# Squares through DRAM from the first step, and the keys' trip issued from ScalarE

## The reference

```python
# attention part (attention-free transformer with a local band)
emb = layernorm(x) + ctx
q, k, v = emb @ wq + bq, emb @ wk + bk, emb @ wv + bv
ek = exp(k - max(k)); ew = exp(w - max(w))        # w: pos_bias inside a band of 64
y = sigmoid(q) * (ew @ (ek * v)) / (ew @ ek)
a = layernorm(y @ wo + bo + emb) * gamma + beta                       # "mid"
ff = relu(a @ w1 + b1) @ w2 + b2
x1 = x + tanh(g_xattn) * (layernorm(ff + a) * gamma + beta)           # "ff"
# channel-mixing part, on xn = layernorm(x1)                          # "fin"
r = sigmoid(mix(xn, mu_r) @ Wr.T); kk = relu(mix(xn, mu_k) @ Wk.T) ** 2
out = x1 + tanh(g_ffn) * r * (kk @ Wv.T)          # mix blends a row with the one before it
```

## Time and profile before

| | |
|---|---|
| time, median of 3 runs | 459.03 us (458.91 to 459.86) |
| the profiled execution | 458.91 us, its span 457.1 us |
| mean granted TensorE clock | 0.996 of full speed |
| TensorE matmul busy | 435.7 us, 95% of the span |
| VectorE, ScalarE, GpSimd busy | 380.0, 286.0, 286.1 us |

### The profile page before, as it was taken

How to read it: one execution, slowest core, us unless ns; L and a number is a source line. 1 busy time by engine, 2 the same in 40 slices (tenths; PEclk the granted TensorE clock), 3 DMA queues, 4 the chain that set the end, 5 groups by cost and what they waited for, 6 DMA issues and landing times.

```text
span 457.1 us, 8142 instructions
## 1 busy us (share of the span) xinstructions
PE 435.7 (95%) x2892; PEld 394.4 (86%) x2892; DVE 380.0 (83%) x768; ACT 286.0 (63%) x449; POOL 286.1 (63%) x227
## 2 busy tenths in 40 slices
PE   8989989997999999999999999999999999998975
PEld 8778789996988888998889888998889898987975
DVE  4998869987597979799798979799788876598887
ACT  3683563835687578745967487745965478537453
POOL 2586847571878657894878657894868453753611
PEclk9999999999899999999999999999999999999999
DMA  8840330442215750448215650445213330011002
GB/s 275 280 138 2 106 103 2 129 125 81 93 55 169 190 150 5 138 128 208 92 56 170 189 145 9 139 127 162 95 58 122 102 101 1 0 48 46 3 0 93
DMA packets 43497, 47.23 MB, mean 103 GB/s; under 512 B 8512, under 2 KB 39744, under 8 KB 43456
## 3 DMA queue, kind: packets, MB, share of 16 engines
q1 hardware_dynamic: 42368, 45.13, 32.6%
q10 hardware_dynamic: 1088, 1.57, 1.0%
HBM read 30.76 MB, written 15.93 MB: 102 GB/s over the span
## 4 chain that ended last, share of the span: by engine, by line
POOL 33%; issue 28%; DVE 15%; PE 11%; ACT 10%; DMA 2%; SPq 0%; POOLq 0%; DVEq 0%; ACTq 0%
PE ps L1806 10%; POOL ek_lo L240 5%; POOL ev_lo L240 5%; POOL x_beta L626 3%; POOL xk_lo L240 2%; POOL emb L352 2%; POOL a_rows L626 2%; POOL rs_mid L618 2%; POOL rs_fin L618 2%; POOL nmr_fin L621 1%; POOL rs_ff L618 1%; DVE ps L948 1%; DVE xk L1031 1%; DVE xr L1031 1%; POOL rs_head L618 1%
## 5 line engine op out<-in xcount | busy, mean ns | idle before, releaser
L1806 PE MATMUL ps<-w_hi,hid_hi 128*128 128x256 f32 x248 | 62.2, 286 | 0.8 <-issue 0.5
L1806 PE MATMUL ps<-w_lo,hid_hi 128*128 128x256 f32 x248 | 61.7, 285 | 0.0
L1595 ACT ACTIVATE hid_hi<-ps,b 128x512 fp32r<-128x512 f32 x60 | 37.7, 681 | 23.6 <-PE ps L1806 23.6
L1806 PE MATMUL ps<-a_hi,w_hi 128*128 128x512 f32 x128 | 50.9, 397 | 1.1 <-DVE hid_lo L1108 1.1
L240 POOL TENSOR_TENSOR ek_lo<-y,ek_hi 128x1024 fp32r<-128x1024 f32 x13 | 36.2, 2788 | 24.5 <-DVE xr L1031 17.8
L1806 PE MATMUL ps<-a_hi,w_lo 128*128 128x512 f32 x128 | 50.7, 396 | 0.0
L1806 PEld LDWEIGHTS ps<-w_hi,hid_hi 128*128 128x128 f32 x248 | 47.6, 192 | 1.7 <-issue 1.2
L1806 PEld LDWEIGHTS ps<-w_lo,hid_hi 128*128 128x128 f32 x248 | 47.5, 192 | 0.3
L1108 DVE SCALAR_TENSOR_TENSOR hid_lo<-ps,neg_b,hid 128x512 fp32r<-128x512 f32 x60 | 41.3, 736 | 3.2 <-ACT hid L1601 3.2
L1601 ACT ACTIVATE hid<-hid_hi,neg_b 128x512 f32<-128x512 f32 x60 | 40.0, 722 | 0.0
L240 POOL TENSOR_TENSOR ev_lo<-res,ev_hi 128x1024 fp32r<-128x1024 f32 x8 | 19.1, 2392 | 29.7 <-ACT ev_hi L1509 29.7
(11 more groups left out here) (278 smaller groups left out, 1407.8 us busy)
## 6 DMA issues: line engine op xcount, KB each, us to landing
x_in<-in_x SPq DMA_DIRECT2D x8, 512.0 KB, 4.6
emb<-in_ctx SPq DMA_DIRECT2D x8, 512.0 KB, 4.3
x_beta<-in_x SPq DMA_DIRECT2D x8, 512.0 KB, 4.3
out<-out_sb SPq DMA_DIRECT2D x7, 512.0 KB, 4.3
key_room<-norm SPq DMA_DIRECT2D x6, 512.0 KB, 2.6
y<-key_room SPq DMA_DIRECT2D x24, 128.0 KB, 2.9
fin_room<-xk SPq DMA_DIRECT2D x6, 512.0 KB, 2.6
out_sb<-fin_room SPq DMA_DIRECT2D x24, 128.0 KB, 2.9
```

The lines of the kernel that those rows point to most:

```text
L1595: act.activation(tile(hi, b, T), bank(relu_pair(n, q), b), ACT.Relu, bias=b1[:, m:m + 1]).then_inc(hid_hi_done, 1)
L1806: return pe.matmul(o, s, m, start=start, stop=stop, skip_group_check=True)
```

## The change

Step 1 now sends the mid rows of batch 1 by squares: TensorE's eight transposes go, and its `queries(2)` move to their place. VectorE turns the mid squares right after their normalisation, and turns the keys' squares after that rather than before. The key squares' round trip is issued from ScalarE's list (`spread_first_keys`), with a semaphore of its own. SP's list of the step now has the load of ctx, the mid trip, the embeddings, the load of x, and the small sums last. VectorE's list of the step is put in another order, `ek_high(2)` on ScalarE comes after `choose_log`, and GpSimd's `stats("ff")` comes ahead of `ek_low(2)`. Three row constants (`bias_rows`, `gamma_t`, `beta_t`) are made by VectorE instead of GpSimd, and two small ones later than before.

```diff
-FIRST_MID = 2
+FIRST_MID = 1
@@ SP, step 1
-                if i == 1:
-                    spread_keys(i + 1)
+                if i == FIRST_MID:
                     load_ctx(i + 2, p)
-                    spread_sums(i + 1)
+                    spread_mid(i)
                     store_emb(i + 2)
                     load_x(i + 3)
                     load_emb(i + 2)
+                    spread_sums(i + 1)
                     load_again(i)
                     spread_fin(i - 1)
@@ GpSimd, prologue and step 1
-            pool.tensor_tensor(bias_rows, bias_rows, beta_t, ALU.add).then_inc(row_const, 1)
-            pool.tensor_scalar(gamma_t, gamma_t, gates[:, 0:1], None, ALU.mult).then_inc(row_const, 1)
-            pool.wait_ge(row_const, 2)
-            pool.tensor_scalar(beta_t, beta_t, gates[:, 0:1], None, ALU.mult).then_inc(row_const, 1)
...
+                stats("ff", b)
                 ek_low(pool, d)
-                stats("ff", b)
                 stats("fin", b)
@@ VectorE, turn_key_squares
-                dve.wait_ge(mid_turned, mid_turns(n - 2))
-                dve.wait_ge(a_scaled_done, 1)
+                dve.wait_ge(mid_turned, mid_turns(max(n - 2, FIRST_MID)))
+                dve.wait_ge(a_scaled_done, 2 if n == FIRST_EK else 1)
@@ VectorE, prologue
             keep_values(1, 3)
+            dve.wait_ge(act_const, 4)
+            dve.tensor_tensor(bias_rows, bias_rows, beta_t, ALU.add).then_inc(dve_const, 1)
+            dve.tensor_scalar(gamma_t, gamma_t, gates[:, 0:1], None, ALU.mult).then_inc(dve_const, 1)
+            dve.wait_ge(dve_const, 2)
+            dve.tensor_scalar(beta_t, beta_t, gates[:, 0:1], None, ALU.mult).then_inc(dve_const, 1)
...
             keys_low(1)
@@ VectorE, step 1
                 head_stats(e)
-                turn_key_squares(d)
                 unit_low(6)
+                unit_low(7)
                 attention_sum(i, p)
                 hidden_low(b, 2)
-                unit_low(7)
                 normalise_mid(i)
+                turn_mid_squares(i)
                 hidden_low(b, 3)
+                turn_key_squares(d)
+                turn_emb_squares(e, p)
+                ff_sum(b, 1 - p)
                 sum_keys(d)
-                a_low(i)
-                ff_sum(b, 1 - p)
-                turn_emb_squares(e, p)
                 ff_stats(b)
+                a_square_low(dve, i)
                 scale_ff(b)
                 keep_values(d)
+                finish_x1(b)
                 weigh_values(d)
+                fin_stats(b)
                 sums_low(d, 0)
                 hidden_low(i, 0)
-                finish_x1(b)
-                fin_stats(b)
                 hidden_low(i, 1)
@@ ScalarE
+            def spread_first_keys():
+                act.wait_ge(ek_turned, FIRST_EK + DC)
+                act.dma_start(key_room.rearrange("(p n) -> p n", p=P), ek_blocks).then_inc(key_room_filled, 16)
+                act.wait_ge(key_room_filled, 16)
+                act.wait_ge(y_lo_done, FIRST_EK)
+                for b in range(NB):
+                    act.dma_start(ek_square[SQ * b:SQ * (b + 1)].rearrange("i (a n) -> i a n", a=NB),
+                                  key_room.rearrange("(a i b n) -> b i a n", a=NB, i=SQ, b=NB)[b]).then_inc(ek_landed, 16)
@@ ScalarE, step 1
                 normalise("mid", i, res)
-                ek_high(d)
+                spread_first_keys()
                 a_high(i)
                 act.wait_ge(act_const, 2)
                 exp_q(d, 2)
                 choose_log()
+                ek_high(d)
                 hidden_high(i, 0)
@@ TensorE, step 1
                     add_hidden(b, 3, rest=False)
-                    pe.wait_ge(norm_done["mid"], TT * (i + 1))
-                    turn(2, norm, mid_turned)
+                    pe.wait_ge(res_done, i + 1)
+                    queries(d, 2)
                     add_hidden(b, 3, high=False)
                 relus_read(NQ * i)
                 values(d, 1)
-                if not has(a):
-                    pe.wait_ge(a_lo_done, i + 1)
-                    queries(d, 2)
                 hidden(i, 0, DC * i)
```

More of the change, by code:

```diff
@@ L168, in flamingo_gated_block @@
         ident_set, const_set, dve_const, act_const = sem("ident_set"), sem("const_set"), sem("dve_const"), sem("act_const")
-        row_const = sem("row_const")
         w_hi_done = sem("w_hi_done")
@@ L210, in flamingo_gated_block @@
                                                                       sem("emb_landed"), sem("fin_landed"))
-        room_filled = sem("room_filled")
+        room_filled, key_room_filled = sem("room_filled"), sem("key_room_filled")
         log_done, guess_done, inverse_done = sem("log_done"), sem("guess_done"), sem("inverse_done")
@@ L292, in stored @@
         def stored(step, place):
-            return 16 * (place if step == 1 else 4 + 5 * (step - 2) + place)
+            return 16 * (place if step == FIRST_MID else 4 + 5 * (step - FIRST_MID - 1) + place)
         def keys_stored(n):
@@ L300, in mid_stored @@
         def mid_stored(n):
-            return stored(n, 2)
+            return stored(n, 1 if n == FIRST_MID else 2)
         def sums_stored(n):
-            return stored(n - 1, 2 if n == FIRST_EK else 3)
+            return stored(n - 1, 3)
         def emb_stored(n):
-            return stored(n - 2, 3 if n == FIRST_EMB else 4)
+            return stored(n - 2, 2 if n == FIRST_EMB else 4)
         def fin_stored(n):
@@ L320, in mid_turns @@
         def mid_turns(n):
-            return n + 1 if n < FIRST_MID else FIRST_MID + DC * (min(n, BATCH - 2) + 1 - FIRST_MID) + (n == BATCH - 1)
+            return 1 + DC * min(n, BATCH - 2) + (n == BATCH - 1)
         def emb_turns(n):
@@ L652, in x_plus_beta @@
             def x_plus_beta(n):
+                pool.wait_ge(dve_const, 3)
                 pool.wait_ge(again_landed, 16 * (n + 1))
@@ L702, in _ @@
             make_emb(pool, 2, 0)
-            pool.wait_ge(row_const, 3)
+            pool.wait_ge(dve_const, 4)
             def first_step(i, p):
@@ L1015, in normalise_mid @@
                 dve.wait_ge(nmr_done["mid"], n + 1)
-                if n > 0 and has(n + 1):
+                if n > FIRST_MID and has(n + 1):
                     dve.wait_ge(room_filled, keys_stored(n + 1))
@@ L1153, in _ @@
             y_low(dve, 0)
-            dve.wait_ge(act_const, 4)
-            dve.tensor_scalar(gates[:, 1:2], gates[:, 2:3], 0.5, None, ALU.mult).then_inc(dve_const, 1)
-            dve.tensor_scalar(one_less_mu, vec[:, C_MUR:C_MUR + 2 * DC], -1.0, 1.0, ALU.mult, ALU.add).then_inc(dve_const, 1)
             first_attention_sum()
@@ L1166, in _ @@
             keep_values(1, 3)
+            dve.wait_ge(act_const, 4)
[3 more added lines that the diff above has]
+            dve.tensor_scalar(beta_t, beta_t, gates[:, 0:1], None, ALU.mult).then_inc(dve_const, 1)
+            dve.tensor_scalar(gates[:, 1:2], gates[:, 2:3], 0.5, None, ALU.mult).then_inc(dve_const, 1)
+            dve.tensor_scalar(one_less_mu, vec[:, C_MUR:C_MUR + 2 * DC], -1.0, 1.0, ALU.mult, ALU.add).then_inc(dve_const, 1)
             keys_low(1)
@@ L1169, in _ @@
             hidden_low(0, 1)
-            dve.wait_ge(dve_const, 2)
-            dve.wait_ge(row_const, 3)
+            dve.wait_ge(dve_const, 5)
             def first_step(i, p):
@@ L1422, in normalise @@
                 act.wait_ge(nmr_done[kind], n + 1)
-                if kind == "mid" and n > 0 and has(n + 1):
+                if kind == "mid" and n > FIRST_MID and has(n + 1):
                     act.wait_ge(room_filled, keys_stored(n + 1))
```

3 lines of the change are left out of this document (removed).

## The result

| | before | after |
|---|---|---|
| time, median (lowest to highest), 4 runs each | 459.25 us (458.91 to 459.86) | 466.11 us (464.41 to 466.58) |
| profiled execution, its span | 458.91, 457.1 us | 465.50, 463.8 us |
| mean granted TensorE clock | 0.996 | 0.992 |
| TensorE matmul busy | 435.7 us (95%) | 438.0 us (94%) |

The ratio is 1.0138, interval [1.0116, 1.0161]: 1.4% slower. The sign was forecast, the size was not: +6.6 us in the profiled pair instead of +1.7, and outside the range of 459.8 to 461.4.

A forecast was written before the change was run, and what follows sets the result against it. Bound: the later of TensorE passing `weigh(2, 1)` and the fin squares landing. TensorE +1.7, squares +1.8, less 0.3 us to spare for TensorE: +1.7 on 458.91 gives 460.6 us, range 459.8 to 461.4.

The forecast's parts named there:

- the fin norm: ScalarE's normalisation of batch 0 at the end of step 1: at 114.6 us, against 112.79 before.
- The front: Stretch up to `keys_low(1)`: not late in the forecast; 1.65 us late in the two-port rival, 462.2 us, chance 0.03.
- the constants: Five small VectorE instructions after `keep_values(1, 3)`: 1.3 us, hidden in idle time, at worst 0.2; held-up rival, chance 0.03.
- the small sums: Last on SP in step 1: land at about 110.1; rival at 113.5 gives 1.7 us more, 462.3, chance 0.07.
- the 1.5 us for `ek_low`: GpSimd's subtraction in step 1 delays VectorE's `finish_x1`: 1.5 us taken, between nothing and 2.4.
- the later of TensorE and squares: Into step 2: TensorE through `weigh(2, 1)` +1.7 us, fin squares' landing +1.8 less 0.3 to spare; the later counts.
- the mid rows' trip: Step 1: `a_hi` half ready at 101.2, TensorE stands from 99.0; covered by the hole if the fin norm comes last.
- the hole: TensorE's 3.3 us wait at the end of step 1, before `weigh(2, 1)`; forecast to move ahead, about as long, 3.2.
- the new order saves nothing: VectorE up to the fin statistics: pieces moved ahead weigh as much as those moved behind; 111.15 against 110.9, +0.3 us.
- the head statistics: GpSimd near 83, beside VectorE's `unit_low(6)`: stretched, so the head norm comes some 1.0 us later.
- the trip of the store: Fin squares' store into step 2: if again 4.1 us they land +1.8; if the usual 2.6, +0.3.
- the low clock: TensorE after the hole: if the clock falls as before, products are again 1.7 us slow; otherwise TensorE is level, +0.1.

The follow-up runs named there:

- e10: e5 with VectorE's fin normalisation and the fin squares' transposes ahead of the last `hidden_low(1, 1)`; 454.59 us, ratio to before 0.9896.
- e11: e10 with `fin_stats` also ahead of `weigh_values` on VectorE; 454.58 us, ratio to before 0.9915.
- e2: The kernel before with only the constants' part of the change, all five made on VectorE after `keep_values(1)`; 461.78 us, ratio to before 1.0056.
- e1: The kernel after with the two small constants (`gates`, `one_less_mu`) back in the prologue; 461.96 us, ratio to before 1.0061.
- e7: The kernel after with the two small constants made first of the five behind `keep_values(1, 3)`; 463.68 us, ratio to before 1.0091.
- e12: e7 with the products of `gamma_t` and `beta_t` made in halves, so the last starts later; 465.50 us, ratio to before 1.0147.
- e3: The kernel after with the small sums' trip ahead of the load of x and the embeddings' reads; 463.49 us, ratio to before 1.0102.
- e4: e1 with the small sums' trip ahead of the embeddings' reads and the load of x behind them; 462.68 us, ratio to before 1.0065.
- e9: e5 with batch 1's mid rows sent by squares, DMAs in the later steps' order, keys from SP; 460.38 us, ratio to before 1.0022.
- e5: The kernel before with only VectorE's step 1 order changed: `finish_x1` before `weigh_values`, `fin_stats` right behind it; 455.64 us, ratio to before 0.9916.
- e6: The kernel before with 12 more identity products on TensorE in the prologue, to shift the instruction packet; 460.40 us, ratio to before 1.0014.

## Why the prediction was wrong, point by point

The forecast had the fin norm at 114.6, and it came at 119.05; behind the norm it missed by 0.5 us. Two terms explain the 4.45 us. The front was 2.87 us late by the constants, which the sum had at nothing. And ScalarE came to the norm 3.05 us after GpSimd had released it, because of the small sums, where the sum said that ScalarE would be waiting by 113.0. Against them stands the 1.5 us for `ek_low`, which was not paid. Both terms had been named, as rivals at 0.03 and 0.07, each added to the forecast alone, and the front at 1.65. They came true together: 460.6, 1.7 for the sums and 2.9 at the front give 465.2, and the profiled execution took 465.50.

- **Right: what sets the end.** The fin squares decided, from their copy to the end it is 333.3 to 333.4 us in all kernels but e10 and e11. The step "the later of TensorE and squares" held: it was the squares. As forecast, TensorE hardly waited before `weigh(2, 1)` in after (0.25 us).
- **Wrong: the constants, "hidden, at worst 0.2".** Measured: 2.7 us alone (e2); in the changed kernel 3.6 to 4.15 (e1), of which 1.35 is a shorter store's trip; 1.9 to 2.4 for the two small ones' place (e7). I costed five instructions by width and didn't ask what GpSimd starts in the same place, except in the sentence on the Trainium skill, which I priced at a chance of 0.03. The price was one instruction held until GpSimd's addition ended, 2.2 us (1.4 of it lost, as VectorE had idled for the rest), and in after and e2 another 1.4 of low clock behind TensorE's wait of 1.8 us. The Trainium skill (SBUF — State Buffer, Who interferes with whom) says it: a `tensor_scalar` can enter a two-port mode, whoever issues first has the ports, and the other is blocked for the whole instruction. The trace agrees, for `one_less_mu` after GpSimd's start (2.33) and before it (0.16), and for `beta_t` likewise (e12, e7). That it is this port, the trace does not show.
- **Wrong: the small sums, a rival at 0.07.** I had them land at 110.1. The store was issued 3.3 us later than I said (106.99 for 103.7), 2.9 of it the late front, and it took 5.7 us to fill for 2.7. That is the stretching that the rival named: 116.36 less 2.87 for the front is its 113.5. Taken out of after, it gives 2.1 to 2.6 us (e3); taken out of e1, nothing in the time and 1.44 us at the norm (e4). My fault was to price each trip at its median of before, where three trips of 512 KB and the load of x now ran into each other. The sign that I had named for it, ScalarE waiting for `sums_raw` past 112, is there (116.36).
- **Wrong: the mid rows' trip, "covered" by the hole.** I laid TensorE's wait for `a_hi` under the hole. That was true of TensorE and beside the point: VectorE waits for the same trip before its remainder of `a` (1.80 us in e9, 0.58 in after), and VectorE is what the fin statistics hang on. e9: 3.1 us on VectorE, 4.7 at the end with a longer trip of the store.
- **Wrong: "the new order saves nothing".** By itself it saves 3.8 us (e5). I summed the moved pieces as if all engines arrived as before; in before, `finish_x1` stood behind `weigh_values`, `sums_low` and `hidden_low(1, 0)`, and so behind ScalarE's copy of the sums, not only behind their own 3 us of work. The new order took them off the chain. I also counted two pairs of transposes as moved ahead, but the keys' pair stood ahead before (82.50).
- **Right by luck: the two together.** The forecast had order and mid squares in one sum, +0.3 us at the statistics. e9 has both: GpSimd gets the statistics at 111.55, less the 1.1 us of its late start 0.5 earlier than before, and the time is 1.06 us over before, with a trip 1.08 longer. A gain and a loss of over 3 us each had cancelled, and neither was seen.
- **Not met: `ek_low` against `finish_x1`.** I took 1.5 us for it, of a possible 2.4. In after it cost nothing, because the keys came 6 us later than I had them (110.42, my 104.45). In e3 and e4, with the keys earlier, `finish_x1` took 1.84 us longer beside it: the mechanism was right, its date wrong.
- **Right: the head statistics** (stretched, 1.1 and 0.6), **the trip of the store** (3.98, forecast "if again 4.1"), and the low clock once more.

The way from before to after in medians, each step against the kernel in front of it: the order -3.8 (e5), the mid squares +4.7 (e9), then +2.3 to e4, then +2.9 to after (from its 465.54) for the late small constants, the late sums and the load of x ahead of the embeddings' reads. The single prices of that last step, 2.7 to 3.6 for the constants (e2, e1) and 0 to 2.1 for the sums (e4, e3), do not simply add. The step of 2.3 from e9 to e4 I did not isolate. It holds the keys' trip from ScalarE, the order of the squares and of SP's trips, the place of `ek_high`, of `unit_low(7)` and of the statistics of "ff", and three constants. Its largest visible part is `finish_x1`, 3.49 us beside `ek_low` in e4 and 1.66 in e9, where the keys come from SP and `ek_low` was long over (96.98 to 99.38).

What stays open is the length of the store's trip, 2.6 to 5.2 us, which is worth up to 2.5 us at the end. With the instruction packet 0.6 to 2.15 us behind the store's issue it was 3.95 to 5.20 (nine kernels), with 2.3 us or more 2.6 to 3.3 (four), and with 0.3 it was 3.35 (e5). The tail of 7 to 9 packets, about one engine's share, goes with the long trips only. It fits an engine that is held up by the instruction packet, but no view names the engine of a packet, and in e9 the packet comes only at 2.15 us. So this stays a correlation; e6 was to move the packet alone and didn't.

## What to carry to other kernels

Find one late event after which all kernels take the same time, and price each edit by what it does to that event, on every engine that waits for a moved transfer and not only on the busiest. A new DMA trip is not worth its median of before once others run beside it. Rivals with different causes can come true together, so work out their sum as well. A tiny instruction moved to "idle" time can cost as much as the neighbour engine's longest one, so look at what runs there and at what waits behind.

## What the runs showed that I had not expected

- The instruction that paid most was one of 4 columns: 2.33 us beside a GpSimd addition, 0.16 started before it. Whether the last constant starts 0.1 us before the addition or just after it decided between e7 (463.7 us) and e12 (465.5).
- The same wait of TensorE of 1.7 to 1.8 us, for `hid_lo` near 67, was followed by 3.41 us at the lower clock in after, e2 and e12, and not in e3.
- The small sums' store, 32 KB, took 1.5 to 5.9 us to fill (SP's rows: 94.99 to 96.45 in e6, 104.21 to 110.12 in e1). The long ones stand beside the trips of keys and embeddings and the load of x.
